# Experts' rows added to residual rows in the output by accumulating scatters, with no last stage

## The reference, cut to what matters

```python
logits = jnp.einsum('btd,ed->bte', x, gate_w)
probs = jax.nn.softmax(logits, axis=-1)
selected_probs, selected_idx = jax.lax.top_k(probs, 2)
selected_probs = selected_probs / (jnp.sum(selected_probs, axis=-1, keepdims=True) + 1e-08)
h = jax.nn.silu(a) * u                       # a, u: x through gate_bank, up_bank (8 experts, 384 hidden)
y_all = jnp.einsum('bteh,ehd->bted', h, down_bank)
...
y = jnp.sum(y_sel * selected_probs[..., None], axis=2)
t = t + y                                    # t: the residual rows, 4096 x 192
```

## Time and profile before

| | us |
|---|---|
| median of 3 runs | 521.87 |
| profiled execution, its time | 525.97 |
| profiled execution, its span (first to last instruction) | 524.2 |
| TensorE matmuls busy | 406.2 (77%) |
| VectorE (DVE) busy | 309.0 (59%) |
| GpSimd (POOL) busy | 242.1 (46%) |
| ScalarE (ACT) busy | 207.4 (40%) |
| routing phase, from its first DVE step | 199.1 |
| expert phase, from GpSimd's first copy | 236.2 |
| last scatter starts | 490.0 |

### The profile page before, as it was taken

The page is one execution under the profiler, slowest core; times in us unless marked ns, Lnnn a source line. Parts: engine busy times, 40 slices in busy tenths (PEclk is TensorE's granted clock), DMA queues, the critical chain, the costliest instruction groups (busy, mean ns, idle before and its releaser), DMA issues.

```text
span 524.2 us, 9292 instructions
## 1 busy us (share of the span) xinstructions
PE 406.2 (77%) x2236; PEld 369.8 (71%) x2237; DVE 309.0 (59%) x764; ACT 207.4 (40%) x481; POOL 242.1 (46%) x353
## 2 busy tenths in 40 slices
PE   5799928468897473385999999999999998999100
PEld 5699827467786462384989999999999997999100
DVE  2266672787875727991655655566655555555164
ACT  3443503413323110472545555555555554555100
POOL 0155542455554510005366666666666665665200
PEclk9999999787757555555999999999999999999655
DMA  7988510022222121101122222222222222222498
GB/s 209 245 200 227 138 57 0 24 63 63 63 63 64 41 80 35 11 1 52 38 73 71 71 72 70 65 71 71 69 67 69 69 71 60 67 70 62 131 352 268
DMA packets 47391, 47.07 MB, mean 90 GB/s; under 512 B 14313, under 2 KB 40332, under 8 KB 47372
## 3 DMA queue, kind: packets, MB, share of 16 engines
q1 hardware_dynamic: 40460, 30.04, 20.8%
q0 software_dynamic: 6912, 16.82, 11.0%
HBM read 32.16 MB, written 14.68 MB: 89 GB/s over the span
## 4 chain that ended last, share of the span: by engine, by line
PE 42%; DMA 5%; issue 3%; SPq 2%; POOL 1%; DVE 1%; ACT 0%; POOLq 0%; ACTq 0%; DVEq 0%
PE moe_ps_y L1149 8%; PE moe_ps_h L1135 4%; PE moe_ps_x L1115 3%; DMA wa_hi<-chosen_rows 3%; PE moe_ps_gt L1124 2%; PE moe_ps_u L1124 2%; PE moe_ps_u L1125 2%; PE moe_ps_u L1127 2%; PE moe_ps_u L1128 2%; PE moe_ps_u L1126 2%; PE moe_ps_gt L1125 2%; PE moe_ps_gt L1126 2%; PE moe_ps_y L1151 2%; PE moe_ps_gt L1128 2%; PE moe_ps_gt L1127 2%
## 5 line engine op out<-in xcount | busy, mean ns | idle before, releaser
L1063 POOL DMA_INDIRECT moe_xt<-rows,moe_idx x72 | 73.1, 1016 | 61.5 <-POOL moe_idx L1060 25.6
L1072 POOL DMA_INDIRECT chosen_rows<-moe_y,moe_idx x72 | 71.4, 991 | 34.4 <-issue 20.3
L1149 PE MATMUL moe_ps_y<-wd,moe_h_hi 128*128 x216 | 72.5, 361 | 1.3 <-DVE moe_h_lo L1280 0.6
L1225 ACT ACTIVATE moe_yy<-moe_ps_y,moe_xt 128x384 f32<-128x384 f32 x72 | 41.9, 582 | 75.5 <-PE moe_ps_y L1149 74.5
L1288 DVE TENSOR_TENSOR moe_y<-moe_yy 128x192 f32<-128x192 f32 x72 | 25.9, 360 | 60.9 <-ACT moe_yy L1225 57.2
L1205 ACT ACTIVATE moe_x_hi<-moe_ps_x 128x256 fp32r<-128x256 f32 x72 | 27.7, 385 | 50.1 <-PE moe_ps_x L1116 48.6
L1264 DVE TENSOR_TENSOR moe_x_lo<-moe_ps_x,moe_x_hi 128x128 fp32r<-128x128 f32 x72 | 21.0, 292 | 44.5 <-issue 27.6
L1149 PEld LDWEIGHTS moe_ps_y<-wd,moe_h_hi 128*128 128x128 f32 x216 | 40.8, 189 | 5.4 <-issue 4.9
L1280 DVE TENSOR_TENSOR moe_h_lo<-moe_ps_h,moe_h_hi 128x384 fp32r<-128x384 f32 x72 | 40.2, 558 | 2.7 <-ACT moe_h_hi L1217 0.5
L1274 DVE TENSOR_TENSOR moe_hid<-moe_ps_u,moe_sg 128x384 f32<-128x384 f32 x72 | 39.5, 548 | 1.2 <-ACT moe_sg L1211 1.2
L1151 PE MATMUL moe_ps_y<-wd,moe_h_lo 128*128 x144 | 36.1, 251 | 0.0
(11 more groups left out here) (185 smaller groups left out, 1173.0 us busy)
## 6 DMA issues: line engine op xcount, KB each, us to landing
wa_hi<-chosen_rows SPq DMA_DIRECT2D x16, 384.0 KB, 6.2
xs<-in_x SPq DMA_DIRECT2D x8, 384.0 KB, 6.0
conv_stage<-in_wgu SPq DMA_DIRECT2D x8, 384.0 KB, 3.8
conv_stage<-in_wgu SPq DMA_DIRECT2D x16, 192.0 KB, 4.7
rows<-attn_xr SPq DMA_DIRECT2D x8, 384.0 KB, 2.7
out<-xs SPq DMA_DIRECT2D x8, 384.0 KB, 6.2
attn_stage<-in_down SPq DMA_DIRECT2D x8, 288.0 KB, 3.3
conv_xta<-in_xT SPq DMA_DIRECT2D x8, 256.0 KB, 4.2
```

Of the source, the lines that this page charges most:

```text
L1063: nc.gpsimd.indirect_dma_start(xt[:, slot, :], None, rows.ap(), bass.IndirectOffsetOnAxis(ap=idx[:, slot, 0:1], axis=0)).then_inc(gathered ...
L1072: nc.gpsimd.indirect_dma_start(chosen_rows.ap(), bass.IndirectOffsetOnAxis(ap=idx[:, slot, 1:2], axis=0), y[:, slot % YR, :], None).then_i ...
L1149: ins = nc.tensor.matmul(both, hi, halves, start=(k == 0), stop=(k == 2))
L1225: nc.scalar.activation(yy[:, s].rearrange("p h c -> p (h c)"), ps_y[:, s, 0:2 * C], ACT.Copy, scale=xt[:, slot, bass.ds(GC + e, 1)]).then_ ...
```

## The change

- The residual rows `xs` are stored to `out` during attention, quad by quad, behind the `rows` stores on SyncE. `out` gets 4 x 128 more rows for padding, which are filled with zeros at the start of attention. The host drops them.
- GpSimd's scatter of tile j now adds `y` to the rows of `out` (`compute_op=ALU.add`). `chosen_rows`, the copies into `idx`, and the last stage are gone.
- A token's two rows are added to the same row of `out`, by two scatters of different experts, so two scatters that may touch the same row must not be in flight together. SyncE orders them through the semaphore `clear`: scatter j goes out after scatter j-2 has landed, and after scatter j-1 too where tile j belongs to another expert than tile j-1. Which tiles these are is computed in routing (`switch`, 16 or 0) and read by SyncE into a register. The first scatters (j up to 4) always wait for j-1.
- GpSimd's loops are written out: 72 scatters and 72 gathers with constants instead of loop registers. GpSimd no longer waits for landings itself.
- Routing: the map needs no sign, so three of the last eight DVE steps go; three small ones for `switch` come before the wait for the map.

```diff
-    chosen_rows = nc.dram_tensor("chosen_rows", [2 * TOKENS + PADS * P, C], F32)
+        switch = keep("switch", [P, TILES_MAX], I32)
...
@@ attention_phase, SyncE
                 sp.dma_start(rows[TOKENS:TOKENS + P, :], zero[:]).then_inc(stored, 16)
+                for k in range(PADS):
+                    at = TOKENS + k * P
+                    sp.dma_start(out[at:at + P, :], zero[:, 0:C]).then_inc(stored, 16)
...
                     sp.dma_start(row_tiles[:, bass.ts(q, QT), C:GC], xr[:, s, :, P:C]).then_inc(rows_out[s], 16)
+                    sp.wait_ge(res_done, made(q))
+                    sp.dma_start(out_tiles[:, bass.ts(q, QT), :], xs[:, bass.ts(q, QT), :]).then_inc(base_out[s], 16)
...
+                    sp.wait_ge(base_out[s], 16 * (QUADS // RING))
@@ routing_phase, DVE
                 ts(tile_exp[:], e_j[:], float(E - 1), None, ALU.min)
+                tt2(e_d[:, 1:TILES_MAX], e_j[:, 1:TILES_MAX], e_j[:, 0:TILES_MAX - 1], ALU.not_equal)
+                then(nc.vector.memset(e_d[:, 0:1], 0.0))
+                ts(switch[:], e_d[:], 16.0, None, ALU.mult)
                 dve.wait_ge(map_done, TILES // HT + HR)
                 then(nc.vector.tensor_copy(slot_v[:], ps_m[:, 0:TILES_MAX]))
                 ts(slot_t[:], slot_v[:], 0.0, no_row[:, 0:1], ALU.is_equal, ALU.mult)
-                stt(out=slot_0[:], in0=slot_v[:], scalar=0.0, in1=no_place[:], op0=ALU.is_equal, op1=ALU.mult)
-                then(stt(out=size[:], in0=slot_v[:], scalar=-1.0, in1=slot_v[:], op0=ALU.mult, op1=ALU.max))
-                then(stt(out=idx_map[:, :, 0], in0=size[:], scalar=-1.0, in1=slot_t[:], op0=ALU.add, op1=ALU.add))
-                stt(out=size[:], in0=size[:], scalar=-1.0, in1=slot_0[:], op0=ALU.add, op1=ALU.add)
-                then(ts(slot_v[:], slot_v[:], 0.0, float(TOKENS), ALU.is_lt, ALU.mult))
-                tt2(idx_map[:, :, 1], size[:], slot_v[:], ALU.add)
+                then(stt(out=slot_0[:], in0=slot_v[:], scalar=0.0, in1=no_place[:], op0=ALU.is_equal, op1=ALU.mult))
+                stt(out=idx_map[:, :, 0], in0=slot_v[:], scalar=-1.0, in1=slot_t[:], op0=ALU.add, op1=ALU.add)
+                stt(out=idx_map[:, :, 1], in0=slot_v[:], scalar=-1.0, in1=slot_0[:], op0=ALU.add, op1=ALU.add)
@@ expert_phase, GpSimd
-                    nc.gpsimd.tensor_copy(idx[:, slot, :], idx_map[:, bass.ds(j, 1), :]).then_inc(idx_done, 1)
-                    pool.wait_ge(idx_done, made(j))
...
+                def scatter(j):
+                    pool.wait_ge(y_done, made(j))
+                    pool.wait_ge(clear, j + 1)
+                    pool.sem_inc(pool_turn, 1)
+                    nc.gpsimd.indirect_dma_start(
+                        out, bass.IndirectOffsetOnAxis(ap=idx_map[:, j, 1:2], axis=0),
+                        y[:, j % YR, :], None, compute_op=ALU.add).then_inc(scattered[j % YR], 16)
+
+                for j in range(AHEAD):
+                    gather(j)
+                for j in range(N):
+                    scatter(j)
+                    if j + AHEAD < N:
+                        gather(j + AHEAD)
@@ expert_phase, DVE: the loop with the adds of L1322 and L1326 goes
@@ expert_phase, SyncE: the loads of L1338 and the stores of L1343 go
+                def landed(j):
+                    sp.wait_ge(scattered[j % YR], 16 * (j // YR) + 16)
+
+                def landed_if_switched(j):
+                    moved = sp.value_load(switch[0:1, j + 1:j + 2], min_val=0, max_val=16)
+                    sp.wait_ge(scattered[j % YR], moved + 16 * (j // YR))
+
+                sp.sem_inc(clear, 1)
+                for j in range(1, N):
+                    if j > 1:
+                        landed(j - 2)
+                    if j <= YR:
+                        landed(j - 1)
+                    else:
+                        landed_if_switched(j - 1)
+                    sp.sem_inc(clear, 1)
+                for j in range(N - YR, N):
+                    landed(j)
@@ kernel
-    out = nc.dram_tensor("out_0", (TOKENS, C), mb.dt.float32, kind="ExternalOutput").ap()
+    out = nc.dram_tensor("out_0", (TOKENS + PADS * P, C), mb.dt.float32, kind="ExternalOutput").ap()
```

More of the change, by code:

```diff
@@ L37 @@
 QUADS = TILES // QT
-PR = 4
 HT, HR = 2, 4
@@ L117, in program @@
                    later)
-        attention_phase(nc, xs, mean, rstd, eye, wqa, wqb, cos_t, sin_t, ga, gb, rows, row_tiles, down, wd, lg)
-        routing_phase(nc, lg, tri, iotas, row_tiles, idx_map, tile_exp)
-        expert_phase(nc, xs, eye, rows, chosen_rows, out, wa_hi, wa_lo, wb_hi, wb_lo, wd, idx_map, tile_exp)
+        attention_phase(nc, xs, mean, rstd, eye, wqa, wqb, cos_t, sin_t, ga, gb, rows, row_tiles, down, wd, lg, out)
+        routing_phase(nc, lg, tri, iotas, row_tiles, idx_map, tile_exp, switch)
+        expert_phase(nc, eye, rows, out, wa_hi, wa_lo, wb_hi, wb_lo, wd, idx_map, tile_exp, switch)
 class Scope:
@@ L482, in transposes, with attention_phase @@
     return ins
-def attention_phase(nc, xs, mean, rstd, eye, wqa, wqb, cos_t, sin_t, ga, gb, rows, row_tiles, down, wd, lg):
+def attention_phase(nc, xs, mean, rstd, eye, wqa, wqb, cos_t, sin_t, ga, gb, rows, row_tiles, down, wd, lg, out):
     with ExitStack() as stack:
@@ L527, in attention_phase @@
         rows_out = [a.sem(f"rows_out{s}") for s in range(RING)]
+        base_out = [a.sem(f"base_out{s}") for s in range(RING)]
+        out_tiles = out[0:TOKENS, :].rearrange("(t p) c -> p t c", p=P)
         last = QUADS // RING - 1
@@ L842, in routing_phase @@
         e_j = a.sb("e_j", [P, TILES_MAX])
-        slot_v, slot_t, slot_0, size = (a.sb(n, [P, TILES_MAX]) for n in ("slot_v", "slot_t", "slot_0", "size"))
+        e_d = a.sb("e_d", [P, TILES_MAX])
+        slot_v, slot_t, slot_0 = (a.sb(n, [P, TILES_MAX]) for n in ("slot_v", "slot_t", "slot_0"))
         hot_b = a.sb("hot_b", [P, HR, 2, HT, P], F32R)
@@ L1042, in expert_phase @@
         scattered = [a.sem(f"scattered{s}") for s in range(YR)]
-        picked, out_stored = ([a.sem(f"{n}{s}") for s in range(PR)] for n in ("picked", "out_stored"))
-        sum_done, total_done = a.sem("sum_done"), a.sem("total_done")
-        idx_done, pool_turn = a.sem("idx_done"), a.sem("pool_turn")
+        clear = a.sem("clear")
+        pool_turn = a.sem("pool_turn")
         xt_done, gate_done, up_done, ht_done, y_mm = (a.sem(n) for n in ("xt_done", "gate_done", "up_done", "ht_done", "y_mm"))
@@ L1054, in _, with gather @@
             def _(pool):
-                pool.sem_inc(idx_done, RING)
-                def gather(i, r):
-                    j, n, slot = XR * i + r, i + r // XR, r % XR
-                    nc.gpsimd.tensor_copy(idx[:, slot, :], idx_map[:, bass.ds(j, 1), :]).then_inc(idx_done, 1)
-                    pool.wait_ge(idx_done, made(j))
+                def gather(j):
+                    slot = j % XR
                     pool.sem_inc(pool_turn, 1)
@@ L1064, in gather @@
                         xt[:, slot, :], None, rows.ap(),
-                        bass.IndirectOffsetOnAxis(ap=idx[:, slot, 0:1], axis=0)).then_inc(gathered[slot], 16)
-                def scatter(i, r):
-                    j, slot = XR * i + r, r % XR
+                        bass.IndirectOffsetOnAxis(ap=idx_map[:, j, 0:1], axis=0)).then_inc(gathered[slot], 16)
+                def scatter(j):
                     pool.wait_ge(y_done, made(j))
+                    pool.wait_ge(clear, j + 1)
                     pool.sem_inc(pool_turn, 1)
                     nc.gpsimd.indirect_dma_start(
[L1073 to L1099, removed]
+                        out, bass.IndirectOffsetOnAxis(ap=idx_map[:, j, 1:2], axis=0),
[6 more added lines that the diff above has]
+                        gather(j + AHEAD)
             @block.tensor
@@ L1315, in _ @@
                     add_parts(n, r - 2)
[L1318 to L1326, removed]
@@ L1328, in _ @@
             @block.sync
             def _(sp):
[L1330 to L1352, removed]
@@ L1353, in _ @@
-                for s in range(PR):
-                    sp.wait_ge(out_stored[s], 16 * QUADS // PR)
+                def landed(j):
[12 more added lines that the diff above has]
+                    sp.sem_inc(clear, 1)
```

15 lines of the change are left out of this document (6 added, 9 removed).

## The result

The changed kernel took **501.28 us** (median of 4 runs, 498.75 to 503.73), the kernel before 521.3. The ratio is 0.9589, with a 95% interval of 0.9552 to 0.9627: 20 us or 4.1% less, where 34.8 us were forecast. The measured time lies in the range, but in the part that the forecast had given to "L toward 5.1" (L is the time from a scatter's start to its landing), and L is not what put it there.

A forecast was written before the change was run, and what follows sets the result against it. It took GpSimd as saturated in the loop, just above TensorE, plus a last stage that only moves data. Terms -28.4 - 4.8 - 1.6 = -34.8 us, off the 521.87 median, gave 487 us; range 472 to 508.

The forecast's parts named there:

- L toward 5.1: Rival: with a longer landing, stalls at start and expert changes eat the loop's gain, 495 to 508 us; chance 0.12.
- part 1: Kernel end: the last stage's loads, adds and stores vanish, the last accumulating scatter ends the kernel; -28.4 us.
- GpSimd becomes the bound again: Rival in the loop: an issue of 2.0 us makes GpSimd's period 3.6, 510 us; chance 0.07 together with pauses.
- part 2: GpSimd's loop: copies and register work go, TensorE becomes the bound; 15.8 us less new waits and a pause, -4.8 us.
- D: Expert loop: distance between scatters when one waits in full for the one before, L + 0.6 = 4.3 us.
- GpSimd as the bound of before: Expert loop before: GpSimd saturated at 3.31 us from scatter to scatter, 0.17 us a tile more than TensorE.
- the rival at L = 6.5: Slower rival: each engine's 8 rows handled one after the other, D' = 7.45 binds inside an expert; +40, 562 us; chance 0.15.
- The tail: Kernel end: last stage of 31.9 us goes, scatter 71 lands at 495.4, kernel ends near 495.8; -28.4 us.
- D': Distance from a scatter's start to the start of the one two later that awaits its landing: 3.7 + 0.95 = 4.65 us.
- Routing and start: Three DVE steps go, three small ones are hidden, GpSimd's first gather no longer stands behind a copy; -1.6 us.
- attention: SyncE's eight more 384 KB stores and four of zeros in attention are covered and cost nothing.
- The rival of cheap accumulation: Reading old rows costs only about 0.4 us more, L 2.7, start and expert stalls vanish; about -46, 476 us; chance 0.20.

The follow-up runs named there:

- the first two experiments: Changed kernel with plain scatters instead of accumulating ones, 481.47 us; changed kernel with odd tiles adding to a second DRAM tensor, no wait for scatter j-1, 487.94 us.
- the repeated profile: The changed kernel, unaltered, profiled once more: tile 0 to 10 took 36.6 us, tile 10 to 71 205.3, the tail 20.7.
- the first experiment: Changed kernel with plain scatters into out in place of accumulating ones, all waits kept: 481.47 us.
- the third experiment: Kernel before with only GpSimd changed: loop written out with constants, index copies gone, plain scatters and last stage kept: 509.00 us.
- its experiment: Kernel before with the further attention stores alone, eight of the residual and four of zeros, to an unread DRAM tensor: 522.34 us, ratio 1.0005.

## Why the prediction was right or wrong

The direction and the range held: the last stage's cost stood in the trace of before, and nothing took its place. The forecast of 487 was 14 us too low. The direction was earned, since the tail alone gives more than the 20 us gained. The place in the range was in part luck: its upper end was there for a longer landing, which did not come, and the loop, which was to give 4.8 us, gave nothing. By its own steps:

- **The step that went wrong** is in part 1: "I take 1.25. GpSimd then needs ... 2.85 us a tile, under TensorE's 3.14." An accumulating scatter is issued in 1.59 us, above the upper bound of 1.5 that I had set, and GpSimd needs 3.18. That is level with TensorE or just above it, and not 0.29 below. The sum treated GpSimd as a queue with slack, and its rival "GpSimd becomes the bound again" started only at an issue of 2.0 and left out the full waits, which cost most on a saturated queue (its terms also give -14 and 508, not -12 and 510). I had taken the bound itself from the page's two kinds of transfer, both at 1.0, and a guess of three descriptors for two; the trace of before held no row for it.
- It made **part 2** wrong in size. With a saturated queue there is no slack of 0.46 to swallow a part of each wait. A change of expert costs 1.2 us and not 0.70, and nothing is regained between changes. Tiles 10 to 71 took 205.4 us as before, where the forecast's terms give 198.2. The traces of the first two experiments part the 7.2 us: without full waits the stretch takes 196.9, so the seven at changes cost 8.5 where 4.9 were forecast; with plain scatters it takes 194.0, so the longer issue and GpSimd's other pauses cost 2.9 where 1.9 were set for a pause; and 194.0 stands against a floor of 191.4 (205.3 less 13.9). That the issue time is what took the slack follows from the row by row timeline and these sums; a run with a shorter issue and the same landing would show it, and there is none. Seven changes and four first waits were named at their right places, and D was 4.4 against 4.3. The eighth, at the start of the padding, was missed. The start's stall was about right: 36.6 us from tile 0 to 10 in the repeated profile against 31.9 in the first experiment, 4.8 where 4.2 were forecast.
- **GpSimd as the bound of before** was right; the third experiment shows it (in-loop waits 15.8 to 1.5 us). Its worth was 13.2 us where 17 were expected of it.
- **L** was right (3.6 for 3.7), and with it the rival at L = 6.5 is out: the 3.18 us from scatter to scatter within an expert show no wait for the one two before.
- **The tail** gave 24.0 us of 28.4. The missing 4.4 us are three: scatter 69 starts 9.0 us after tile 71's first load in place of 7.5, behind its full wait; scatter 71 follows it by 5.96 us where D' was 4.65 (0.30 and 0.6 add up to 0.90 there, not 0.95); and the end comes 5.7 us after its start in place of 4.1, because GpSimd's drain ends 1.8 us after SyncE has seen the last landing (499.9 to 501.7).
- **Routing and start** -1.1 of -1.6; **attention** 0, shown by its experiment.
- **The rival of cheap accumulation** is wrong in its price too. In the stretch from 300 to 420 us, in the loop, GpSimd's DMA queue took this share of the 16 engines, before and after (packets, MB, share):

```profile
q0 software_dynamic: 3453, 8.40, 24.0%
```

```profile
q0 software_dynamic: 6903, 8.40, 44.4%
```

That is 28.8 us for 73 transfers before, and 53.3 us for 72 after. The ends of the kernels, where only scatters run, part them: five plain ones from 481 to 492.5 us before, three accumulating ones from 490 to 502 after:

```profile
q0 software_dynamic: 240, 0.49, 13.0%
```

```profile
q0 software_dynamic: 432, 0.30, 24.2%
```

1.50 us for five is 0.30 us of each engine for a plain scatter; 2.90 us for three is 0.97 for an accumulating one, 3.2 times as much, in three times the packets (144 for 48). A gather takes 0.51 (17.1% of the 18 us from 233 to 251 for the first six of the changed kernel), and 36 of each give the loop's 53.3 us. The Trainium skill ("Collectives: The Full Stack", "The bandwidth ceiling: the fold count and why AG ≠ RS ≠ AR") gives half rate for a ring's reducing transfers, because of the second source read. It has the direction; this case's rows show more than that. Neither decided the time here, since the engines were less than half busy.

## What to carry to other kernels

Add up what each in-order queue issues for one step, the idle gaps ahead of its transfers too, before calling an engine that is at nine tenths the bound; here the queue with no wait for data in its period was the bound, at six tenths busy. When a change moves work onto such a queue, or a wait in front of it, the price is the full one, and an unmeasured issue time deserves a range that crosses the point where the bound changes. An ordering wait costs what the queue behind it has no slack for: nearly nothing with plain scatters here, 13 us with accumulating ones. Gathering as far ahead as the buffers allow took 5 of these back for one constant.

## What the runs showed of the hardware that was not expected

- An accumulating indirect scatter of 128 rows of 768 bytes took GpSimd 1.59 us to issue and 3.6 us to land; a plain one 0.99 and 2.4.
- GpSimd's drain ended some 5.4 us after the start of its last accumulating scatter (once 6.6), 1.7 us or more after SyncE had seen it land. In the kernel before it ended 4.8 us after the last plain one, and the last stage hid it. What the drain waits for, and why the last scatter starts a further 1 us late after its release (496.20, where SyncE's register load ran at 493.7 and its last increment at 494.4), was not tried.
- GpSimd's pause of 3.22 us at 436.86 does not come just anywhere: the kernel before with further stores has the same 3.22 us before the same gather, that of tile 59. The changed kernel has none there, but two smaller ones: the one at scatter 6, and 0.8 us of idle time in place of 0.3 ahead of scatter 37, which its repeat shows too. Their cause stays open.
